# An RNN and an LSTM on one core: x, h0 and bias go out first, weight peaks and splits are put elsewhere among the first 13 steps, and the RNN's split form begins at step 12

## The chip, the core and the metric

The kernel runs on one core of a Trainium2 chip. A core has five engines with queues of their own: TensorE (PE; its weight loads are shown as PEld), VectorE (DVE), ScalarE (ACT), GpSimd (POOL) and SyncE (SP), which here only issues DMAs. ACT issues some DMAs too. An engine works its instructions in order and waits where one asks for a semaphore that has not come. The metric is the device time of one execution in microseconds.

## The reference, cut to what matters

```python
def step(prev_h, xw):                      # RNN, B=32, T=128, D=H=512
    next_h = jnp.tanh(prev_h @ Wh + xw)    # xw = x @ Wx + b
    return (next_h, next_h)
...
def step(carry, xw_t):                     # LSTM, four gates of 512
    prev_h, prev_c = carry
    a = xw_t + prev_h @ Wh
    i, f, o = sigmoid(a[:, :H]), sigmoid(a[:, H:2*H]), sigmoid(a[:, 2*H:3*H])
    g = jnp.tanh(a[:, 3*H:])
    next_c = f * prev_c + i * g
    next_h = o * jnp.tanh(next_c)
    return ((next_h, next_c), next_h)
...
x = x + rnn(x, h0)       # y
x = x + lstm(y, h0)      # c starts at zero
```

## The kernel before

**Steps and lag.** The program is written out by hand, one block for each engine, and each block runs a loop over k = 0 to 133. Iteration k holds step k of the RNN and step k-6 of the LSTM (`LAG = 6`), so the LSTM reads the RNN's sum y six steps later. x is loaded, turned and scaled in groups of four steps (`TG = 4`): group g is steps 4g to 4g+3. The order within an iteration is the order of the calls at the end of each block, and tables with k as the key (`W_HIGH_AT`, `W_LOW_AT`, `PEAK_AT`, `SCALE_AT` and so on) say in which iteration the work on the weights is done.

**Two forms of a product.** In the first steps the products use float32 operands as they were loaded. Later each float32 operand is replaced by two float16 parts, a high and a low one, and a product is three: high by high, high by low, low by high. The LSTM's recurrent product is split from step 1 on (`recurrent_l`), its input product from step 8 on (`product_l`, `S1 = 8`). The RNN's products are split from step `R0` on (`product_r16`, `recurrent_r16`); before, R0 = 8. In the split form one half of the RNN's result comes out in other rows of PSUM, so ACT copies it (`other_half_out`), POOL adds the bias (`add_bias_r16`) and DVE sums (`rnn_add_r16`), and the new h has to be split by ACT and DVE (`rnn_h_hi`, `rnn_h_lo`). In the float32 form DVE adds PSUM and bias directly (`rnn_add`).

**What splitting needs.** Each split takes a scale, a power of two, from a bound on the largest element. For the weights a reduction of each of the four chunks of Wh and Wx of the LSTM (128 x 2048 floats each) gives one column: before, ACT does all eight with Abs and a sum along the row (`weight_peak`). When four are there, TensorE turns them (`turn_peaks`), DVE takes the maximum and puts it on a diagonal (`spread`), TensorE spreads it to all partitions (`spread_peaks`), and DVE works out the scale (`weight_scale`, a chain of short operations). Then ACT writes the high part of each chunk (`weight_high`: `whl_hi`, `wxl_hi`) and DVE the low part (`weight_low`: `whl_lo`, `wxl_lo`). The RNN's weights (`wxr`, `whr`) and each group of x and y are treated likewise. In the profile the exchange goes through `ps_pk`, `peak_col` and `peak_diag`.

**What waits for what.** The recurrent product of LSTM step 1 waits for all four `whl_lo`; the input product of step 8, in iteration 13, waits for all four `wxl_lo` and for y's split (`y_lo`). Step 0 of the LSTM multiplies the raw weights (L729, L737) and needs all eight chunks loaded. The RNN's step r goes TensorE (L788, L798), DVE sum (L634), ACT tanh (L423), DVE turn (L658).

**Loads.** ACT issues x's group 0 as four DMAs, then h0, then the RNN's bias; SP issues `wxr_raw`, `whr_raw`, x group 1, `whl_raw` 0 and 1, x group 2, `whl_raw` 2 and 3, x group 3, four `wxl_raw`, the LSTM's bias and further x.

Of the kernel before, what the change touches and what calls it, by code (L numbers as in the profile page):

```python
# [27 lines left out]
def rnn_lstm_kernel(nc, x, h0, WxR, WhR, bR, WxL, WhL, bL, out):  # L28
# [10 lines left out]
    with ctx:  # L39
# [302 lines left out]
        def _(act):  # L342
            load_x(act, 0)
            act.dma_start(h0n[:, :], h0.rearrange("b (j u) -> j b u", j=J)).then_inc(s_h0, DMA)
            act.dma_start(bias_r[:, :], bass.AP(tensor=bR.tensor, offset=0, ap=[[P, J], [0, B], [1, P]])).then_inc(s_bias_r, DMA)
# [79 lines left out]
            for k in range(END):  # L425
                n, t = k // TG, k % TG
                if 0 <= k - LAG:
                    gate_values(k - LAG)
# [13 lines left out]
                for of, chunk in W_HIGH_AT.get(k, []):  # L442
                    weight_high(of, chunk)
                for of, chunk in W_PEAK_AT.get(k, []):
                    weight_peak(of, chunk)
                for of in R_HIGH_AT.get(k, []):
                    rnn_weight_high(of)
# [478 lines left out]
```

## Time and profile before

| | us |
|---|---|
| median of 3 runs (lowest, highest) | 925.95 (925.73, 926.93) |
| the profiled execution | 926.05 |
| its span in the trace | 924.2 |
| TensorE busy (share of the span) | 866.3 (94%) |
| DVE busy | 754.4 (82%) |
| ACT busy | 409.4 (44%) |
| POOL busy | 233.6 (25%) |

The shares are means over two very different parts. In the last 85% of the span TensorE is busy almost throughout; the first 137 us hold nearly all of its idle time. So the rows to read are those of the start: which engine each one waits for, and when the loads land.

### The profile page before, as it was taken

Reading aid. Unit: us, or ns where it says so; the run is one execution under the profiler, and the core shown is the slowest. Engines: PE = TensorE matmul, PEld = TensorE weight load, DVE = VectorE, ACT = ScalarE, POOL = GpSimd, SP = SyncE. Lnnn points to the kernel's source line nnn. Section 1 sums busy time; section 2 is a strip of 40 time slices with the busy share of each in tenths; the row PEclk is TensorE's granted clock in tenths of the full one; section 3 lists DMA queues with packets and bytes.
Section 4 is the critical chain, followed back from the end, with each engine's and each line's share of the span. In section 5 each row is a group of like instructions: output and inputs, shape, how many; then the busy total and the mean of one; then the engine's idle time right before and its main releaser. Section 6 shows DMA issues by size and latency. Waiting matters only on the chain.

```text
span 924.2 us, 42085 instructions
## 1 busy us (share of the span) xinstructions
PE 866.3 (94%) x18460; PEld 512.9 (55%) x18460; DVE 754.4 (82%) x1985; ACT 409.4 (44%) x1090; POOL 233.6 (25%) x511
## 2 busy tenths in 40 slices
PE   3768779999999999999999999999999999999996
PEld 2524346666565556556555655565556555656542
DVE  3665778888888888888888888888888888888875
ACT  0744444444444444444444544444445444444431
POOL 0221112222222222222222222222222222222210
PEclk9879899999999999999999999999999999999999
DMA  9800000111110001010000010111000100000000
GB/s 312 253 1 2 24 6 23 26 26 26 26 25 24 12 20 26 25 27 26 26 21 19 15 26 26 26 26 26 18 21 17 26 14 15 15 15 15 15 13 13
DMA packets 39328, 30.36 MB, mean 33 GB/s; under 512 B 4328, under 2 KB 37864, under 8 KB 37864
## 3 DMA queue, kind: packets, MB, share of 16 engines
q1 hardware_dynamic: 38304, 27.28, 10.6%
q8 instruction: 144, 2.36, 1.1%
q10 hardware_dynamic: 840, 0.39, 0.2%
q14 instruction: 40, 0.33, 0.1%
HBM read 19.27 MB, written 8.39 MB: 30 GB/s over the span
## 4 chain that ended last, share of the span: by engine, by line
PE 83%; DVE 7%; ACT 4%; issue 3%; DMA 2%; POOL 0%; ACTq 0%; POOLq 0%; DVEq 0%
PE ps_l L750 34%; PE ps_l L774 31%; PE ps_r L813 8%; PE ps_r L830 8%; DMA bias_r<-in_L_cond_b 2%; PE ps_l L763 1%; DVE whl_lo L580 1%; DVE pre_l L593 1%; ACT gates L411 1%; ACT wxl_hi L386 1%; DVE h_hi L615 1%; PE ps_l L729 1%; ACT tanh_c L418 1%; DVE h_lo L625 0%; DVE c L604 0%
## 5 line engine op out<-in xcount | busy, mean ns | idle before, releaser
L774 PE MATMUL ps_l<-wxl_hi,whl_raw 128*32 128x512 f16 x3840 | 251.6, 379 | 2.9 <-issue 2.9
L774 PEld LDWEIGHTS ps_l<-wxl_hi,whl_raw 128*32 128x32 f16 x3840 | 105.6, 97 | 105.1 <-issue 8.3
L307 POOL TENSOR_TENSOR xb<-xb,h_l 128x128 f32<-128x128 f32 x128 | 59.4, 464 | 356.5 <-DVE h_l L621 356.5
L750 PE MATMUL ps_l<-whl_hi,hT_hi 128*32 128x512 f16 x2032 | 134.2, 384 | 11.3 <-DVE whl_lo L580 8.7
L330 POOL TENSOR_TENSOR yT<-xT,hT_r 128x128 f32<-128x128 f32 x128 | 62.8, 491 | 284.5 <-DVE hT_r L658 284.5
L750 PE MATMUL ps_l<-whl_lo,hT_hi 128*32 128x512 f16 x2032 | 133.5, 383 | 0.0
L750 PE MATMUL ps_l<-whl_hi,hT_lo 128*32 128x512 f16 x2032 | 132.6, 381 | 0.0
L593 DVE SCALAR_TENSOR_TENSOR pre_l<-ps_l,g_products,bias_l 128x256 f32<-128x256 f32 x240 | 105.1, 480 | 25.7 <-PE ps_l L750 19.0
L774 PE MATMUL ps_l<-wxl_lo,whl_raw 128*32 128x512 f16 x1920 | 125.8, 379 | 0.0
L641 DVE SCALAR_TENSOR_TENSOR pre_r<-ps_r,g_products,xr 64x128 f32<-64x128 f32 x240 | 84.0, 350 | 41.9 <-POOL xr L320 36.7
L423 ACT ACTIVATE h_r<-pre_r 128x128 f32<-128x128 f32 x128 | 39.6, 310 | 140.6 <-DVE pre_r L641 115.2
L398 ACT ACTIVATE xr<-ps_r,g_products 64x128 f32<-64x128 f32 x120 | 43.8, 365 | 120.5 <-PE ps_r L813 120.5
L407 ACT ACTIVATE hT_r_hi<-hT_r,g_inverses 128x128 f16<-128x128 f32 x120 | 48.2, 402 | 103.6 <-DVE hT_r L658 103.6
L750 PEld LDWEIGHTS ps_l<-whl_lo,hT_hi 128*32 128x32 f16 x2032 | 55.7, 98 | 55.7 <-issue 2.3
L750 PEld LDWEIGHTS ps_l<-whl_hi,hT_lo 128*32 128x32 f16 x2032 | 55.5, 98 | 55.3 <-issue 1.6
L411 ACT ACTIVATE gates<-pre_l 128x256 f32<-128x256 f32 x128 | 53.4, 417 | 73.4 <-DVE pre_l L593 70.2
L625 DVE SCALAR_TENSOR_TENSOR h_lo<-h_l,g_inverses,h_hi 128x128 f16<-128x128 f32 x120 | 77.9, 649 | 4.2
L774 PEld LDWEIGHTS ps_l<-wxl_lo,whl_raw 128*32 128x32 f16 x1920 | 52.7, 97 | 51.4
L750 PEld LDWEIGHTS ps_l<-whl_hi,hT_hi 128*32 128x32 f16 x2032 | 54.1, 98 | 43.0 <-DVE whl_lo L580 9.0
L418 ACT ACTIVATE tanh_c<-c 128x128 f32<-128x128 f32 x128 | 39.7, 310 | 62.1 <-DVE c L604 62.1
L320 POOL TENSOR_TENSOR xr<-xr,bias_r 128x128 f32<-128x128 f32 x120 | 55.1, 459 | 45.4 <-ACT xr L399 42.2
L316 POOL TENSOR_TENSOR xb<-xb,h_r 128x128 f32<-128x128 f32 x128 | 61.0, 476 | 0.0
(97 smaller groups left out, 1286.0 us busy)
## 6 DMA issues: line engine op xcount, KB each, us to landing
out<-xb SPq DMA_DIRECT2D x128, 64.0 KB, 1.8
xb<-in_x SPq DMA_DIRECT2D x124, 64.0 KB, 2.1
whl_raw<-in_L_cond_Wh SPq DMA_DIRECT2D x4, 1024.0 KB, 14.2
wxl_raw<-in_L_cond_Wx SPq DMA_DIRECT2D x4, 1024.0 KB, 18.5
wxr_raw<-in_L_cond_Wx SPq DMA_DIRECT2D x1, 1024.0 KB, 5.4
whr_raw<-in_L_cond_Wh SPq DMA_DIRECT2D x1, 1024.0 KB, 8.0
xb<-in_x ACTq DMA_DIRECT2D x4, 64.0 KB, 8.2
bias_l<-in_L_cond_b SPq DMA_DIRECT2D x4, 64.0 KB, 16.6
```

The costliest lines, as they stand in the source:

```text
L307: nc.gpsimd.tensor_tensor(xb[g % NX][:, t, :], xb[g % NX][:, t, :], h_l[s % 2][:, :], ALU.add).then_inc(out_done, 1)
L316: nc.gpsimd.tensor_tensor(xb[g % NX][:, t, :], xb[g % NX][:, t, :], h_r[r % 2][:, :], ALU.add).then_inc(y_done, 1)
L320: nc.gpsimd.tensor_tensor(xr[r % 2][:, :], xr[r % 2][:, :], bias_r[:, :], ALU.add).then_inc(r16_sum, 1)
L330: nc.gpsimd.tensor_tensor(yT[g % 2][:, :, t, :], xT[g % 2][:, :, t, :], hT_r[:, :, :], ALU.add).then_inc(yT_done, 1)
L411: nc.scalar.activation(gates[:, 0:2 * P], pre_l[:, 0:2 * P], ACT.Sigmoid).then_inc(lstm_act, 1)
L593: nc.vector.scalar_tensor_tensor(out=pre_l[:, cols], in0=ps_l[s % 2][:, cols], scalar=unscale_l(s), in1=bias_l[:, cols], op0=ALU.mult, op1 ...
L625: nc.vector.scalar_tensor_tensor(out=h_lo[:, :], in0=h_l[s % 2][:, :], scalar=factor, in1=h_hi[:, :], op0=ALU.mult, op1=ALU.subtract).then ...
L641: last = nc.vector.scalar_tensor_tensor(out=pre_r[half, :], in0=ps_r[r % 2][half, m * P:(m + 1) * P], scalar=unscale_r[half, g:g + 1], in1 ...
L750: last = nc.tensor.matmul(ps_l[s % 2][quarter(j), :], (hT_hi, hT_lo)[h_part][:, k, :], gate_slice(whl[w_part][k], j), start=False, stop=(h ...
L774: last = nc.tensor.matmul(ps_l[s % 2][quarter(j), :], y16[y_part][g % 2][:, k, t * B:(t + 1) * B], gate_slice(wxl[w_part][k], j), start=(y ...
L813: last = nc.tensor.matmul(ps_r[r % 2][quarter(2 * p + c), 0:2 * P], (hT_r_hi, hT_r_lo)[h_part][:, 2 * p + k, :], quadrant_of_r16(wr[OF_H][ ...
L830: last = nc.tensor.matmul(ps_r[r % 2][quarter(2 * p + c), 0:2 * P], x16[x_part][g % 2][:, 2 * p + k, t * B:(t + 1) * B], quadrant_of_r16(w ...
```

## The change

SP now issues two of the four DMAs of x's group 0 and the RNN's bias ahead of all matrices; ACT issues the other two and h0. R0 becomes 12. The LSTM weights' bounds are shared: chunks 1 and 3 of Wh and chunk 3 of Wx get a maximum on DVE (`weight_max`), the other five stay on ACT (`weight_bound`, the former `weight_peak`). The two scale exchanges of the RNN's groups become one, `scales` loses its partial forms, and its first batch is exchanged in iteration 9, not 5. The spreading matmul of Wh's peaks stands ahead of step 0's recurrent product. ACT's high parts of Wx move ahead of the gates' next use, one of them a step earlier, and DVE's low parts now stand right behind `hidden` (the LSTM's state) and ahead of `rnn_add`, where before they closed the iteration. `whr`'s split moves from k = 3 and 4 to k = 7 and 8.

```diff
-R0 = 8
+R0 = 12
...
-        EXCHANGE = {OF_H: 1, OF_X: 3}
-        R_SCALE_AT = 1
-        SCALE_AT = {OF_H: 4, OF_X: 8}
+        EXCHANGE = {OF_H: 1, OF_X: 2}
+        R_SCALE_AT = 2
+        SCALE_AT = {OF_H: 4, OF_X: 7}
...
+            load_x(sp, 0, (0, 1))
+            sp.dma_start(bias_r[:, :], bass.AP(tensor=bR.tensor, offset=0, ap=[[P, J], [0, B], [1, P]])).then_inc(s_bias_r, DMA)
             sp.dma_start(wr_raw[OF_X][:, :], WxR.rearrange("(p k) n -> p (k n)", k=J)).then_inc(s_wr[OF_X], DMA)
...
-            load_x(act, 0)
+            load_x(act, 0, (2, 3))
             act.dma_start(h0n[:, :], h0.rearrange("b (j u) -> j b u", j=J)).then_inc(s_h0, DMA)
-            act.dma_start(bias_r[:, :], bass.AP(tensor=bR.tensor, offset=0, ap=[[P, J], [0, B], [1, P]])).then_inc(s_bias_r, DMA)
...
+            def weight_max(of, k):
+                dve.wait_ge((s_whl, s_wxl)[of][k], DMA)
+                nc.vector.tensor_reduce(peaks[:, J * of + k:J * of + k + 1], raw[of][k][:, :], mybir.AxisListType.X, ALU.max,
+                                        apply_absolute_value=True).then_inc(w_peaked[of], 1)
...
                     hidden(k - LAG)
...
+                for of, chunk in W_LOW_AT.get(k, []):
+                    weight_low(of, chunk)
+                if k in R_LOW_AT:
+                    rnn_weight_low(R_LOW_AT[k])
                 if LAG <= k < R0:
                     rnn_add(k)
...
-                for of, chunk in W_LOW_AT.get(k, []):
-                    weight_low(of, chunk)
```

DVE in the first steps, before: from the turn of x's group 1 in iteration 0 to the sum of RNN step 2.

```order
L466 STREAM_TRANSPOSE xT<-xb 128x4x4x32
L570 TENSOR_REDUCE peaks<-whr_raw 128x1
L634 TENSOR_TENSOR pre_r<-ps_r,bias_r 128x128
L658 STREAM_TRANSPOSE hT_r<-h_r 128x128
L490 TENSOR_REDUCE peak_col<-ps_pk 2x1
L494 TENSOR_SCALAR peak_diag<-ident,peak_col 2x2
L634 TENSOR_TENSOR pre_r<-ps_r,bias_r 128x128
```

The same stretch of DVE after, to the sum of RNN step 3:

```order
L475 STREAM_TRANSPOSE xT<-xb 128x4x4x32
L643 TENSOR_TENSOR pre_r<-ps_r,bias_r 128x128
L667 STREAM_TRANSPOSE hT_r<-h_r 128x128
L579 TENSOR_REDUCE peaks<-whr_raw 128x1
L643 TENSOR_TENSOR pre_r<-ps_r,bias_r 128x128
L667 STREAM_TRANSPOSE hT_r<-h_r 128x128
L499 TENSOR_REDUCE peak_col<-ps_pk 2x1
L503 TENSOR_SCALAR peak_diag<-ident,peak_col 2x2
L574 TENSOR_REDUCE peaks<-whl_raw 128x1
L643 TENSOR_TENSOR pre_r<-ps_r,bias_r 128x128
```

The maximum of `whr_raw` and the exchange stand one RNN step later, and a maximum of `whl_raw` has come in ahead of the sum of step 3.

DVE in iterations 10 and 11, before, from `hT_lo` of LSTM step 4 to the cell of step 5 (numbers behind a name are buffer numbers):

```order
L628 STREAM_TRANSPOSE hT_lo<-h_lo 128x128
L641 SCALAR_TENSOR_TENSOR pre_r<-ps_r0,g_products,xr0 64x128 x2
L471 SCALAR_TENSOR_TENSOR xT_lo1<-xT1,g_inverses,xT_hi1 128x512
L478 TENSOR_REDUCE peaks<-xb6 128x1
L658 STREAM_TRANSPOSE hT_r<-h_r0 128x128
L580 SCALAR_TENSOR_TENSOR wxl_lo1<-wxl_raw1,w_scale,wxl_hi1 128x2048
L593 SCALAR_TENSOR_TENSOR pre_l<-ps_l1,m_unscale,bias_l 128x256 x2
```

And after:

```order
L637 STREAM_TRANSPOSE hT_lo<-h_lo 128x128
L561 TENSOR_TENSOR g_products<-g_power,factors 128x6x2
L564 RECIPROCAL g_inverses<-g_products 128x6x2
L589 SCALAR_TENSOR_TENSOR wxl_lo1<-wxl_raw1,w_scale,wxl_hi1 128x2048
L643 TENSOR_TENSOR pre_r<-ps_r0,bias_r 128x128
L480 SCALAR_TENSOR_TENSOR xT_lo1<-xT1,g_inverses,xT_hi1 128x512
L487 TENSOR_REDUCE peaks<-xb6 128x1
L667 STREAM_TRANSPOSE hT_r<-h_r0 128x128
L602 SCALAR_TENSOR_TENSOR pre_l<-ps_l1,m_unscale,bias_l 128x256 x2
```

The low part has moved from behind the RNN's turn to ahead of the RNN's sum, which has its float32 form here.

ACT from the tanh of the LSTM's cell in iteration 9, before, to the gates of iteration 10:

```order
L418 ACTIVATE tanh_c<-c 128x128
L398 ACTIVATE xr1<-ps_r1,g_products 64x128
L399 ACTIVATE xr1<-ps_r1,g_products 64x128
L423 ACTIVATE h_r1<-pre_r 128x128
L407 ACTIVATE hT_r_hi<-hT_r,g_inverses 128x128
L386 ACTIVATE wxl_hi0<-wxl_raw0,w_scale 128x2048
L411 ACTIVATE gates<-pre_l 128x256
```

ACT after, from the RNN's tanh of iteration 8 to the one of iteration 9:

```order
L423 ACTIVATE h_r0<-pre_r 128x128
L365 ACTIVATE yT1<-yT1,m_scale 128x512
L386 ACTIVATE wxl_hi0<-wxl_raw0,w_scale 128x2048
L411 ACTIVATE gates<-pre_l 128x256
L413 ACTIVATE gates<-pre_l 128x128
L414 ACTIVATE gates<-pre_l 128x128
L418 ACTIVATE tanh_c<-c 128x128
L386 ACTIVATE wxl_hi1<-wxl_raw1,w_scale 128x2048
L386 ACTIVATE wxl_hi2<-wxl_raw2,w_scale 128x2048
L423 ACTIVATE h_r1<-pre_r 128x128
```

`wxl_hi0` stands one iteration earlier, and two more high parts are done where one was, ahead of the RNN's tanh.

## Rows read from the trace of the kernel before

**Rows 1.** Stretches: bounds and length, busy us (instructions) by engine, clock, DMA share, GB/s

```profile
31.70:42.00 10.30, 7.97 (x99) 4.64 (x99) 6.68 (x9) 7.34 (x8) 3.76 (x4) 0.67 1.02 261
...
53.50:62.20 8.70, 0.01 (x3) 0.00 (x0) 7.74 (x14) 4.71 (x5) 5.18 (x3) 0.69 0.00 0
62.20:137.50 75.30, 61.11 (x929) 31.13 (x933) 46.82 (x120) 30.03 (x63) 11.57 (x25) 0.88 0.04 9
137.50:203.00 65.50, 65.50 (x1460) 42.26 (x1452) 57.24 (x153) 30.40 (x86) 18.22 (x41) 1.00 0.11 27
```

**Rows 2.** TensorE in order of time: start, us, line, operation [idle before <- releaser]

```profile
62.25 1.90 PE L750 MATMUL ps_l<-whl_hi,hT_hi 128*32 128x512 f16 x16 [8.74 <-DVE whl_lo L580]
...
133.59 1.05 PE L774 MATMUL ps_l<-wxl_hi,whl_raw 128*32 128x512 f16 x16 [2.87 <-issue]
...
137.48 1.05 PE L750 MATMUL ps_l<-whl_hi,hT_hi 128*32 128x512 f16 x16
```

**Rows 3.** DMA issues at 1.19, 7.18, 7.65, 16.1: last number us to landing

```profile
whr_raw<-in_L_cond_Wh SPq DMA_DIRECT2D x1, 1024.0 KB, 8.0
...
whl_raw<-in_L_cond_Wh SPq DMA_DIRECT2D x1, 1024.0 KB, 15.2
...
whl_raw<-in_L_cond_Wh SPq DMA_DIRECT2D x1, 1024.0 KB, 18.3
...
wxl_raw<-in_L_cond_Wx SPq DMA_DIRECT2D x1, 1024.0 KB, 22.6
```

**Rows 4.** Queues, 4 to 6 us: packets, MB, share of engines; then DVE's turn of h0

```profile
q1 hardware_dynamic: 110, 0.77, 94.9%
q10 hardware_dynamic: 109, 0.05, 8.5%
...
16.68 0.40 DVE L455 STREAM_TRANSPOSE hT_r<-h0n 128x128 f32<-128x128 f32 x1 [5.06 <-DMA h0n<-in_cond]
```

**Rows 5.** Operations in order of time, all engines, 17 to 58 us

```profile
17.29 2.25 DVE L570 TENSOR_REDUCE peaks<-wxr_raw 128x1 f32<-128x2048 f32 x1
...
24.56 1.89 ACT L381 ACTIVATE whl_lo<-whl_raw 128x2048 bf16<-128x2048 f32 x1
...
27.40 0.13 DVE L528 TENSOR_SCALAR r_peak<-ps_pk 128x2 f32<-128x2 f32 x1
...
28.81 0.23 DVE L500 TENSOR_SCALAR factors<-r_scale,factors 128x2 f32<-128x2 f32 x1
...
37.20 4.86 PE L729 MATMUL ps_l<-whl_raw,h0T 128*32 128x512 f32 x29
...
37.52 1.24 DVE L478 TENSOR_REDUCE peaks<-xb 128x1 f32<-128x512 f32 x2
...
42.41 0.16 DVE L506 TENSOR_REDUCE w_peak<-ps_pk 128x1 f32<-128x4 f32 x1 [0.96 <-PE ps_pk L846]
...
43.64 0.27 DVE L634 TENSOR_TENSOR pre_r<-ps_r,bias_r 128x128 f32<-128x128 f32 x1
...
44.29 0.44 DVE L658 STREAM_TRANSPOSE hT_r<-h_r 128x128 f32<-128x128 f32 x1 [0.38 <-ACT h_r L423]
...
44.66 1.19 DVE L466 STREAM_TRANSPOSE xT<-xb 128x512 f32<-128x512 f32 x1
...
51.22 0.75 DVE L593 SCALAR_TENSOR_TENSOR pre_l<-ps_l,bias_l 128x256 f32<-128x256 f32 x2
...
54.52 0.31 DVE L628 STREAM_TRANSPOSE hT_lo<-h_lo 128x128 f16<-128x128 f16 x1
...
57.42 4.78 DVE L580 SCALAR_TENSOR_TENSOR whl_lo<-whl_raw,w_scale,whl_hi 128x2048 f16<-128x2048 f32 x2
```

**Rows 6.** Waits, 88 to 137 us (us in total, times, longest); and ACT's high part

```profile
DVE wxl_lo L580 <- ACT wxl_hi L386: 8.8, 4, 2.4
...
107.70 1.99 ACT L386 ACTIVATE wxl_hi<-wxl_raw,w_scale 128x2048 f16<-128x2048 f32 x1
```

**Rows 7.** An add on POOL while DVE writes `wxr_lo`

```profile
31.79 2.47 POOL L330 TENSOR_TENSOR yT<-xT,hT_r 128x128 f32<-128x128 f32 x1 [3.35 <-DVE hT_r L658]
```

More of the change, by code:

```diff
@@ L429, in _ @@
                     cell_tanh(k - LAG)
+                    for of, chunk in W_BOUND_AT.get(k, []):
+                        weight_bound(of, chunk)
+                    if k in R_HIGH_AT:
+                        rnn_weight_high(R_HIGH_AT[k])
+                    if k >= SCALE_AT[OF_X] + 2:
+                        for of, chunk in W_HIGH_AT.get(k, []):
+                            weight_high(of, chunk)
                 if R0 <= k < T:
@@ L441, in _ @@
                     y_scale(Y_SCALE_AT[k])
[L442 to L447, printed above, removed]
+                if k < SCALE_AT[OF_X] + 2:
+                    for of, chunk in W_HIGH_AT.get(k, []):
+                        weight_high(of, chunk)
+                if k < LAG:
+                    for of, chunk in W_BOUND_AT.get(k, []):
+                        weight_bound(of, chunk)
+                if k < LAG and k in R_HIGH_AT:
+                    rnn_weight_high(R_HIGH_AT[k])
         @block.vector
@@ L547, in x_power, with scales @@
                                         ALU.bitwise_and).then_inc(done, 1)
-            def scales(i, kinds, done, step):
+            def scales(i, done, step):
                 first, count = BATCHES[i]
-                cols, shape = slice(first, first + count), [P, kinds.stop - kinds.start, count]
-                nc.vector.tensor_tensor(g_products[:, kinds, cols], g_power[:, cols].unsqueeze(1).broadcast_to(shape),
-                                        factors[:, kinds].unsqueeze(2).broadcast_to(shape), ALU.mult).then_inc(done, 1)
+                cols, shape = slice(first, first + count), [P, 6, count]
+                nc.vector.tensor_tensor(g_products[:, :, cols], g_power[:, cols].unsqueeze(1).broadcast_to(shape),
+                                        factors[:, :].unsqueeze(2).broadcast_to(shape), ALU.mult).then_inc(done, 1)
                 dve.wait_ge(done, step + 1)
-                nc.vector.reciprocal(g_inverses[:, kinds, cols], g_products[:, kinds, cols]).then_inc(done, 1)
+                nc.vector.reciprocal(g_inverses[:, :, cols], g_products[:, :, cols]).then_inc(done, 1)
             def x_scale(i):
@@ L666, in _ @@
                     rnn_add(k)
+                    for of, chunk in W_LOW_FIRST_AT.get(k, []):
+                        weight_low(of, chunk)
                     rnn_turn(k)
+                    if k == 0:
+                        turn_x(1)
+                    if k in R_PEAK_AT:
+                        rnn_weight_peak(R_PEAK_AT[k])
+                    if k == R_SCALE_AT:
+                        spread(EXCHANGE_R, 2)
+                    if k - 1 == R_SCALE_AT:
+                        rnn_weight_scale()
+                    if k in W_MAX_AT:
+                        weight_max(*W_MAX_AT[k])
+                    if k == SCALE_AT[OF_H]:
+                        spread(EXCHANGE[OF_H], J)
+                        weight_scale(OF_H)
                 if 0 <= k - LAG:
```

118 lines of the change are left out of this document (49 added, 69 removed).

## The prediction

> **What bounds the kernel now.** I read the table of stretches first [rows 1]. From 137.5 to 203 us TensorE is busy all of 65.50 us at the full granted clock; before that it is not. From 62.2 to 137.5 it works 61.11 of 75.30 us at a mean clock of 0.88, and from 53.5 to 62.2 it does nothing. So the program has a TensorE-bound tail and a start in which others decide. The next view, TensorE's own rows [rows 2], gives the marks: LSTM step 1 begins its recurrent product at 62.25, after 8.74 us in which it waited for the last `whl_lo`; the first split input product (step 8) begins at 133.59, and the recurrent product of step 8 at 137.48. From there both kernels issue the same work in the same order, at TensorE's pace. The question is thus when that product starts; 924.2 - 137.48 = 786.7 us follow it unchanged. The landing rows [rows 3] and the durations [rows 5] let me walk the new order up to it. I count iterations k as the code does: k carries RNN step k and LSTM step k-6.
>
> **1. x, h0 and bias first.** Before, h0 is only turned at 16.68, after DVE waited 5.06 us for it [rows 4], though its descriptors were out by 4.06. The two rows of the DMA queues from 4 to 6 us say why: queue 10 (ACT's) and queue 1 (SP's) moved 109 and 110 packets, one for one, and queue 1's have 8 KB. After the change h0 is issued third instead of fifth on ACT's queue, some 1.2 us earlier, and the matrices some 1.5 us later (three small issues of about 0.5 us ahead of them). x0 no longer shares its way. I take h0 landed at about 10, when `whr_raw` lands too: it was 1.19 + 8.0 = 9.2 [rows 3], and I add 0.8, between 0 (x0, h0 and bias use time in which the DMA engines were idle) and the 1.5 of the issue. RNN step 0 then multiplies at 10 to 11.3 rather than behind 16.68: 6 us sooner. But most of that is not kept. `whl_raw2` landed at 7.18 + 15.2 = 22.4, and the same bytes are ahead of it; with +0.3 (bounds 0 and +1.5) it lands at 22.7, and ACT's bound on it sits in front of the tanh of RNN step 3. So the first term is a landing: 22.7.
>
> **2. Peaks and scales of the LSTM weights, k = 3 to 4.** From 22.7: ACT's bound 1.89 + 0.19 [rows 5] to 24.8. The tail of RNN step 3 (tanh, turn) 0.75 to 25.55. The scale of the RNN weights, six dependent short operations from 27.40 to 29.04 in the rows, 1.65 to 27.2. `weight_max` of chunk 3 on DVE: the nearest row is the reduction of `wxr_raw`, 2048 columns too, 2.25, to 29.45 (`whl_raw3` is there from 7.65 + 18.3 + 0.3 = 26.3). Chunk 1's maximum, done by 23.9, ends before ACT does. Moving three of eight peaks to DVE thus costs DVE 2.25 here and saves ACT 2.08; before, all four of Wh were on ACT, one after another. The tail of RNN step 4 takes 1.1 (43.64 to 44.73), to 30.55; largest of a column and diagonal 0.55, to 31.1; TensorE spreads it, 0.4; the weight scale takes 1.3 (42.41 on), to 32.9. The spread now stands ahead of step 0's product, so the scale no longer waits for it: 42.41 becomes 31.6.
>
> **3. Step 0 and the splits of Wh, k = 4 to 6.** TensorE multiplies step 0's recurrent part from 31.6. In the rows it took 5.2 with the granted clock at 0.67 around it [rows 1, 5]; TensorE has been waiting since about 26.7 for two microseconds and more, so I keep the slow value, to 36.8 (at full clock 3.6, as the same 32 matmuls of the input part took; at 1.2 GHz throughout twice that, 7.3). RNN step 5: product 0.9 to 37.7, sum to 38.05. Meanwhile DVE does `wxr_lo` (33.0 to 35.3), which is hidden. Then `whl_lo0` 2.35 to 40.4, turn to 40.8, `whl_lo1` and `whl_lo2` to 45.6 with 0.2 of waiting (ACT's three high parts follow each other at 1.92 from 39.0). `wxl_raw3` lands at 16.1 + 22.6 + 0.3 = 39.0, so step 0's input product ends at 42.2 and is hidden. LSTM step 0 takes from 51.22 to 54.83 in the rows, 3.6: to 49.2. `whl_lo3` 2.35: 51.6. **The recurrent product of step 1 starts at 51.6, not 62.25: 10.65 us sooner.**
>
> **4. The splits of Wx, k = 7 to 13.** Step 1's product waits 4.1 us before it starts, so I keep the slow clock and 5.1 (2.7 at full clock): DVE's cell 1 at 56.75. From here I give the starts of the cell on DVE. Cell to `hT_lo` is 3.7.
> k=7: `weight_max` 2.25, RNN sum, x peak 0.65 (1.24 for two), turn, to 64.1; TensorE's own work, with the turned peaks waiting for 62.75, ends step 2's product at 65.8. Cell 2 at 65.85.
> k=8: 3.7, weight scale 1.35, `whr_lo` 2.3, then sum, peak, turn 1.4: cell 3 at 74.6.
> k=9: ACT does `wxl_hi0` ahead of the gates: +1.5; spread 0.5, `wxl_lo0` 2.35, x turn 1.15, sum, peak, turn 1.4, x power 0.6: cell 4 at 85.75 (11.15).
> k=10: 3.75, scales 0.35, low part 2.35, sum, `xT_lo` 0.7, peak, turn: 94.25.
> k=11: 3.75 + 2.35 + 1.35: 101.7.
> k=12: 3.75, spread 0.5, low part 2.35 to 108.3; RNN's first split sum, `y_lo`, turn, x power: cell 7 at 111.2. Input product of step 8 starts behind `y_lo` at 110.2; RNN's low half comes at 113.35 and TensorE reaches the recurrent product of step 8 at **114.4**.
> What makes this shorter is one wait: before, each of k=9 to 12 had ACT's high part (1.99) after ACT's `hT_r_hi`, and DVE idle for it: four waits, 2.4 the longest, 8.8 us in all [rows 6]. Now the high part lies a step ahead of the low part. R0 = 12 takes four steps off the longer path through ACT, GpSimd and the low half (0.4 + 0.35 of DVE each), and costs TensorE about 0.5 us in each of four steps, which DVE's 7.5 to 11 us a step hide.
>
> GpSimd and DVE: an add on GpSimd that takes 0.46 alone took 2.47 beside `wxr_lo` [rows 7]. At k=12 the bias add starts at 106.5, inside `wxl_lo3`, so I end it at 108.7 instead of 107.0; since DVE itself is free at 108.3, that is 0.4 in the sum. In the Trainium skill, SBUF — State Buffer, section SBUF: two separate sides, the pair of ports that the two share is a lock held for a whole instruction, and the loser stands still. By that rule the long operations next to the LSTM state speak against this change; by it the time is 903.0, without it 902.6.
>
> **The sum.** 137.48 - 114.4 = 23.1. The profiled execution: 924.2 + 1.85 around it = 926.05, 0.1 over the median of 925.95. 926.05 - 23.1 = 903.0.
>
> **The rivals.**
> *A, the walk as it stands*: 901 to 906. For it: every length is a row and 137.5 on is full.
> *B, the granted clock stays up at step 0 and at step 1*: 1.6 and 2.4 less, 899.0. For it: less waiting than now. Against: it fell in each of the early stretches with a wait of some 2 us or more.
> *C, h0 late*: if it again takes 12.6 us from its descriptors (16.68 - 4.06), it lands at 15.5; RNN step 0 starts 5 us later than I say, the slack of about 0.6 at the tanh of step 3 is gone and that comes at 29.3: +4.2, 907.2. For it: the one-for-one row. Against: x0 is out of its queue's way. The Trainium skill, DMA: Bandwidth & Descriptors, section Queues, rings and completion order, has the DMA engines take turns between queues by packets, so that small ones beside a matrix stay slow even when issued first.
> *D, more waits than I walked*: loads late by the full 1.5 (+1.2), step 0 at 1.2 GHz throughout (+2.1) and one more clock fall inside k = 7 to 12 (+2.5): up to 909.
> *E, half the gain*: another engine's queue (ACT at k = 6 and 7, with 4 to 6 us of long work before the tanh) delays every early step: about 915.
> *F, slower*: the loop from step 8 on locks with DVE later than TensorE. There are 120 steps, so from 0.19 us each the 23 us are gone; at 0.3 the time is 903.0 + 36 = 939. Against: 65.50 of 65.50 busy, and DVE 57.24 of it: it can catch up 1 us in a step.
>
> **How the numbers follow.** A 0.50, B 0.15, C 0.15, D 0.14, E 0.03, F 0.02, and 0.01 that it all ends even. About 0.2% is what a measurement of this kernel can tell from no change. A, B, C and most of D hold over 8 in 10: from 898.5 to 909.5. Faster 0.97, same 0.01, slower 0.02.
>
> **What would show it.** h0 turned at about 10; tanh of RNN step 3 at 25 right behind ACT's bound; the weight scale at 31.6 ahead of step 0's product; step 1's product at 51.6; no DVE wait for `wxl_hi`; cells 7.5 to 11 us apart; step 8's recurrent product at 114.4 with TensorE full after it. Wrong if a long wait of DVE on ACT stands in k = 6 to 9, if landings move by over 2 us, or if TensorE is not full after 115.

## The result, and the profile after

| | before | after |
|---|---|---|
| median of 4 runs (lowest, highest), us | 926.44 (925.73, 926.96) | 899.19 (897.55, 900.53) |
| ratio (95% interval) | | 0.9706 (0.9687 to 0.9724) |
| the profiled execution, us | 926.05 | 900.53 |
| its span, us | 924.2 | 898.7 |
| TensorE busy, us (share) | 866.3 (94%) | 861.6 (96%) |

The change saves 27 us. The forecast was 903.0 (898.5 to 909.5): 3.8 above the median, 2.5 above the profiled execution. The runs of the changed kernel lie up to 3 us apart, and the profiled one is the slowest of the four, so the traces are compared below from marks inside them, and the medians where a time is meant.

The stretches of the changed kernel (bounds and length, busy us (instructions) by engine, granted clock, DMA share, GB/s) answer to [rows 1]:

```profile
26.00:37.00 11.00, 7.53 (x92) 3.96 (x96) 8.16 (x20) 5.02 (x6) 1.76 (x4) 0.69 1.04 369
47.50:53.00 5.50, 1.07 (x44) 0.80 (x39) 4.84 (x11) 4.94 (x8) 0.56 (x1) 0.99 0.01 1
53.00:108.00 55.00, 52.82 (x900) 27.35 (x900) 45.57 (x109) 23.78 (x44) 10.20 (x19) 0.97 0.05 12
112.00:203.00 91.00, 91.00 (x2028) 58.98 (x2023) 80.27 (x213) 42.24 (x120) 25.52 (x57) 1.00 0.10 26
```

From 112 us TensorE is busy all of the time, as it was before from 137.5. Between LSTM step 1 and step 8 it now works 52.82 of 55.00 us at a clock of 0.97, where it had worked 61.11 of 75.30 at 0.88.

TensorE's rows in order of time (start, us, line, operation, idle before and its releaser) answer to [rows 2]:

```profile
13.34 1.94 PE L809 MATMUL ps_r<-whr_raw,hT_r 128*32 128x128 f32 x32 [1.15 <-DMA whr_raw<-in_L_cond_Wh]
...
33.29 4.90 PE L740 MATMUL ps_l<-whl_raw,h0T 128*32 128x512 f32 x32
...
52.97 1.90 PE L761 MATMUL ps_l<-whl_hi,hT_hi 128*32 128x512 f16 x16 [4.43 <-DVE whl_lo L589]
...
108.10 1.05 PE L785 MATMUL ps_l<-wxl_hi,whl_raw 128*32 128x512 f16 x16 [0.43 <-DVE whl_raw L492]
...
111.99 1.05 PE L761 MATMUL ps_l<-whl_hi,hT_hi 128*32 128x512 f16 x16
```

Step 1's recurrent product starts at 52.97 instead of 62.25, and its wait is 4.43 instead of 8.74. Step 8's starts at 111.99 instead of 137.48: 25.49 us sooner, and the profiled executions are 25.52 apart. Nothing was gained or lost after that mark. Of the 25.5 us, 9.3 are there by step 1 and 16.2 come between step 1 and step 8 (59.0 us instead of 75.2). Three kernels of the experiments have the same code up to step 1 (R0 = 16, and the two with the parts of Wx put back); there its product starts at 50.89, 51.21 and 50.59, so 52.97 is a late case.

The landings (last number: us from issue to landing) answer to [rows 3]; `whr_raw` is issued at 2.87, the second `whl_raw` pair from 9.82 on. Behind them stands the turn of h0 on DVE, which answers to [rows 4], and ACT's bound on chunk 2 with the tanh of RNN step 3 behind it:

```profile
wxr_raw<-in_L_cond_Wx SPq DMA_DIRECT2D x1, 1024.0 KB, 7.8
whr_raw<-in_L_cond_Wh SPq DMA_DIRECT2D x1, 1024.0 KB, 10.4
```

```profile
8.31 0.40 DVE L464 STREAM_TRANSPOSE hT_r<-h0n 128x128 f32<-128x128 f32 x1 [3.41 <-DMA h0n<-in_cond]
```

```profile
24.50 1.91 ACT L381 ACTIVATE whl_lo<-whl_raw 128x2048 bf16<-128x2048 f32 x1 [1.96 <-DMA whl_raw<-in_L_cond_Wh]
...
26.41 0.29 ACT L423 ACTIVATE h_r<-pre_r 128x128 f32<-128x128 f32 x1
```

h0 is there at 8.31 instead of 16.68, but now `whr_raw` is what RNN step 0 waits for, and it lands at 2.87 + 10.4 = 13.3, not at 9.2. `wxr_raw`, ahead of it, already took 7.8 us instead of 5.4. The tanh of step 3 stands right behind ACT's bound, at 26.41 (30.98 before).

### The profile page after: what moved, and what is told of

Same layout as the page of the kernel before. It is cut to its first block, busy times and chain, and to the rows that moved or that the text cites. A ratio compares the mean times of both kernels' runs of the same rounds, so it can differ in the third digit from the quotient of the medians.

```text
span 898.7 us, 42172 instructions
## 1 busy us (share of the span) xinstructions
PE 861.6 (96%) x18524; PEld 510.3 (57%) x18524; DVE 755.4 (84%) x1977; ACT 398.7 (44%) x1071; POOL 228.4 (25%) x507
## 4 chain that ended last, share of the span: by engine, by line
PE 84%; DVE 8%; issue 2%; ACT 2%; DMA 2%; SPq 1%; POOL 0%; POOLq 0%; ACTq 0%; DVEq 0%
PE ps_l L761 35%; PE ps_l L785 31%; PE ps_r L824 8%; PE ps_r L841 8%; DMA whl_raw<-in_L_cond_Wh 2%; DVE pre_l L602 1%; ACT gates L411 1%; DVE whl_lo L589 1%; DVE h_hi L624 1%; DVE h_lo L634 1%; SPq L263 1%; ACT tanh_c L418 1%; DVE c L613 1%; DVE fc L609 1%; DVE ig L611 1%
## 5 line engine op out<-in xcount | busy, mean ns | idle before, releaser
L331 POOL TENSOR_TENSOR yT<-xT,hT_r 128x128 f32<-128x128 f32 x128 | 58.6, 458 | 295.5 <-DVE hT_r L667 295.5
L650 DVE SCALAR_TENSOR_TENSOR pre_r<-ps_r,g_products,xr 64x128 f32<-64x128 f32 x232 | 81.1, 350 | 34.8 <-POOL xr L321 29.8
## 6 DMA issues: line engine op xcount, KB each, us to landing
whl_raw<-in_L_cond_Wh SPq DMA_DIRECT2D x4, 1024.0 KB, 14.2
whr_raw<-in_L_cond_Wh SPq DMA_DIRECT2D x1, 1024.0 KB, 10.4
```

Of the source, the lines that this page charges most:

```text
L331: nc.gpsimd.tensor_tensor(yT[g % 2][:, :, t, :], xT[g % 2][:, :, t, :], hT_r[:, :, :], ALU.add).then_inc(yT_done, 1)
L650: last = nc.vector.scalar_tensor_tensor(out=pre_r[half, :], in0=ps_r[r % 2][half, m * P:(m + 1) * P], scalar=unscale_r[half, g:g + 1], in1 ...
```

## The experiments

Of the causes, I had named one wait (`wxl_lo` on `wxl_hi`, 8.8 us [rows 6]), the loads, the spread put ahead and the shared bounds; to R0 = 12 I had given 0.4 + 0.35 us of DVE a step, some 3 us in all, and had taken its cost on TensorE to be hidden. The runs undo each alone, or do one alone. Not tried alone are the move of `whr`'s split to k = 7 and 8 and the joining of the RNN's exchanges. Where a saving "from the mark" is given, it is the time from the recurrent product of step 1 to DVE's cell of step 8 in the trace (the cell starts with the add that reads the gates' sums, `pre_l`): 78.3 us before, 62.4 after. It leaves out the loads' scatter. Differences to the changed kernel are of the medians. The kernel before ran beside each group of experiments too, at 925.83, 926.97 or 926.38 us; by the ratios to it the differences come out up to 0.9 us otherwise (2.0 in place of 2.9 for the bounds on ACT).

### The loads, undone and alone

The changed kernel with the old loads:

```diff
-            load_x(sp, 0, (0, 1))
-            sp.dma_start(bias_r...)
-            load_x(act, 0, (2, 3))
+            load_x(act, 0)
             act.dma_start(h0n...)
+            act.dma_start(bias_r...)
```

> The changed kernel with the loads of x's group 0, h0 and bias as before (all on ACT's queue, matrices first on SP's). My theory: h0 is turned at about 16.7 again instead of 8.3, RNN step 0's recurrent product starts at about 17.2 instead of 13.3, and since only some 0.7 us of slack stand ahead of ACT's bound on chunk 2 of Wh, 3 to 4 us of that reach the end: 902 to 903 against the changed kernel's 899.2. Rival (the landing of chunk 2 sets the start whatever the RNN does): tanh of RNN step 3 stays within 1 us of 26.4, time 898 to 900. Rival (the load order is the main thing): over 8 us back, 907 or more.

Measured: 903.16 (902.26 to 905.2), ratio 0.9754 (0.9739 to 0.9768). That is 4.0 over the changed kernel, a little above the 902 to 903 that were expected. The other way round, the kernel before with the new loads and nothing else:

> The kernel before with the new order of loads alone (x's group 0 on both queues, bias on SP, nothing else). My theory: the RNN starts 4 us sooner and all of it is kept up to step 1 of the LSTM, since that start bounded the kernel before: 922 us (921 to 924) against 926.4. Rival (loads are throughput-bound and give nothing): 925.5 to 926.5. Rival (main thing): 915 or less.

Measured: 920.81 (918.7 to 923.81), ratio 0.9944 (0.9927 to 0.996): 5.0 less than the kernel before beside it, and just below the 921 to 924 expected. So the loads are worth 4 to 5 us either way. With the old loads in the changed kernel, RNN step 0 waits for h0 as before (TensorE's rows):

```profile
17.23 1.94 PE L808 MATMUL ps_r<-whr_raw,hT_r 128*32 128x128 f32 x32 [3.21 <-DVE hT_r L463]
...
56.81 1.90 PE L760 MATMUL ps_l<-whl_hi,hT_hi 128*32 128x512 f16 x16 [4.43 <-DVE whl_lo L588]
```

Step 0 starts 3.9 us later than in the changed kernel and step 1 of the LSTM 3.8 us later: the whole delay is handed on. Against the three earlier cases named above (RNN step 0 at 11.6 to 12.2) both delays are 5.0 to 6.2 us. In the kernel before with new loads, step 1's product comes at 56.78 instead of 62.25, with the same 8.72 of waiting for `whl_lo`.

### R0 = 12 alone

```diff
-R0 = 8
+R0 = 12
...
-        BATCHES = [(RG, 2)] + [(g, 4) for g in range(4, NG, 4)]
+        BATCHES = [(G1, 2)] + [(g, 4) for g in range(4, NG, 4)]
```

(in the kernel before; the two waits on `x_peaked` count from G1 too.)

> The kernel before with R0 = 12 alone (groups 2 and 3 of x still scaled in one early batch, which is then batch 2, 2). My theory: in k = 8 to 11 the RNN's float32 sum does without ACT's copies, the bias add, ACT's and DVE's split of h, 1.5 to 2 us of each of four iterations that DVE bounds: 918 to 921 against 925.8. Rival (TensorE pays 0.5 us a step and the rest is hidden): 925.5 to 928.

Measured: 915.82 (914.89 to 917.5), ratio 0.9883 (0.9868 to 0.9897). That is 11.1 us less than the kernel before beside it (926.97), against the 5 to 8 expected. Iteration 9 shows how. DVE in the kernel before, from the cell of step 3 on:

```profile
87.78 0.87 DVE L593 SCALAR_TENSOR_TENSOR pre_l<-ps_l,m_unscale,bias_l 128x256 f32<-128x256 f32 x2
...
93.25 0.71 DVE L641 SCALAR_TENSOR_TENSOR pre_r<-ps_r,g_products,xr 64x128 f32<-64x128 f32 x2 [1.47 <-POOL xr L320]
...
98.41 2.35 DVE L580 SCALAR_TENSOR_TENSOR wxl_lo<-wxl_raw,w_scale,wxl_hi 128x2048 f16<-128x2048 f32 x1 [2.36 <-ACT wxl_hi L386]
```

and the same operations with R0 = 12 alone:

```profile
83.60 0.88 DVE L593 SCALAR_TENSOR_TENSOR pre_l<-ps_l,m_unscale,bias_l 128x256 f32<-128x256 f32 x2 [1.28 <-PE ps_l L750]
...
87.93 0.29 DVE L634 TENSOR_TENSOR pre_r<-ps_r,bias_r 128x128 f32<-128x128 f32 x1 [0.33 <-PE ps_r L798]
...
90.49 2.42 DVE L580 SCALAR_TENSOR_TENSOR wxl_lo<-wxl_raw,w_scale,wxl_hi 128x2048 f16<-128x2048 f32 x1 [0.27 <-ACT wxl_hi L386]
```

From the cell to the start of `wxl_lo0` it was 10.63 us and is 6.89. The wait for POOL (1.47) becomes one of 0.33 for TensorE, because no copy by ACT and no add by POOL lie between product and sum. The wait for `wxl_hi` falls from 2.36 to 0.27, though ACT's high part stands where it stood: ACT no longer has to do `hT_r_hi` ahead of it. The stretches from cell to cell (k = 9, then the five of k = 8 to 12 together as 58.42 us before and 47.41 after; of the kernel before, then of this one) give the rest:

```profile
87.78:100.79 13.01, 11.23 (x176) 5.75 (x168) 8.73 (x20) 4.54 (x9) 1.91 (x4) 1.00 0.17 42
...
sum 58.42, PE 44.53 PEld 22.92 DVE 39.23 ACT 24.77 POOL 9.36; mean PE 8.91 PEld 4.58 DVE 7.85 ACT 4.95 POOL 1.87
```

```profile
83.60:92.83 9.23, 9.23 (x160) 4.36 (x156) 8.00 (x17) 3.42 (x6) 3.09 (x3) 1.00 0.18 45
...
sum 47.41, PE 40.07 PEld 21.67 DVE 35.90 ACT 19.54 POOL 9.63; mean PE 8.01 PEld 4.33 DVE 7.18 ACT 3.91 POOL 1.93
```

DVE's work falls by 3.3 us, as the 0.4 + 0.35 a step had it, and its idle time from 19.2 to 11.5, by 7.7, for which I had no term. By iteration, from k = 8 to 12, the five are 3.1, 3.8, 2.8, 1.2 and 0.1 us shorter. Of the 8.8 us for which `wxl_lo` waited, 5.0 are left with R0 = 12 alone.

Two things stand outside these stretches. LSTM step 1's product already starts at 60.68 instead of 62.25: DVE's low part of x's group 2, with a wait of 0.68 ahead of it, is gone from iteration 6. And at step 8's input product the granted clock fell, which it had not done in the kernel before. Here are TensorE's rows for it, first of the kernel before with the new loads, then of this one:

```profile
128.14 1.05 PE L776 MATMUL ps_l<-wxl_hi,whl_raw 128*32 128x512 f16 x16 [3.50 <-issue]
```

```profile
121.54 1.90 PE L774 MATMUL ps_l<-wxl_hi,whl_raw 128*32 128x512 f16 x16 [3.50 <-issue]
```

Both waited 3.50 us for the same product; the clock was 1.00 from 128 to 130 us in the first and 0.50 from 122 to 124 in the second.

### How long the float32 form should last

```diff
-R0 = 12
+R0 = 16
```

> The changed kernel with R0 = 16. In iterations 12 to 15 the RNN's products stay float32: 1.75 us of TensorE a step instead of 1.31, and no split of h. My theory: at k = 12 DVE still bounds and saves 1 us, at k = 13 to 15 TensorE bounds and pays 0.44 each plus the first product: 899.2 to 900.5. Rival (the float32 form is the better one as long as it can be had, as it was in k = 8 to 11): 897 or less.

Measured: 899.58 (898.71 to 900.96), ratio 0.9713 (0.9694 to 0.9731). No difference that the runs can tell. From step 1's product to the end its trace takes 846.1 us instead of 845.7. Past step 12 the low parts of Wx are done, and from 112 us TensorE is full in the changed kernel.

### The low and the high parts of Wx, where they stood before

First only the low parts, in the changed kernel: those of k = 9 to 12 back at the end of the iteration.

```diff
-                for of, chunk in W_LOW_AT.get(k, []):
+                for of, chunk in W_LOW_AT.get(k, []) if k < 9 else []:
                     weight_low(of, chunk)
...
                     x_power(BATCH_AT.index(k))
+                for of, chunk in W_LOW_AT.get(k, []) if k >= 9 else []:
+                    weight_low(of, chunk)
```

> The changed kernel with DVE's four low parts of Wx back at the end of their iterations (k = 9 to 12), while ACT's high parts keep their early place. My theory: what the change gains there is the wait of DVE for ACT, not the place of the low part, so DVE has the same sum of work in each iteration and the time stays within 1 us of 899.2. Rival (the place right behind the LSTM state is what gains): each of four iterations pays 1 us or more, 903 or more. Rival (the place costs, since it holds back the RNN): 898 or less.

Measured: 903.34 (903.12 to 903.54), ratio 0.9752 (0.974 to 0.9765): 4.1 us more than the changed kernel, where I expected none. Each part of it has a row. At k = 10 ACT's high part of x was covered by DVE's low part, and is waited for now; at k = 12 the last low part comes to stand behind `y_lo`, so TensorE waits for it (DVE's rows, then TensorE's two, of this kernel):

```profile
88.60 0.75 DVE L480 SCALAR_TENSOR_TENSOR xT_lo<-xT,g_inverses,xT_hi 128x512 f16<-128x512 f32 x1 [0.71 <-ACT xT_hi L356]
...
106.18 2.62 DVE L589 SCALAR_TENSOR_TENSOR wxl_lo<-wxl_raw,w_scale,wxl_hi 128x2048 f16<-128x2048 f32 x1
```

```profile
108.91 1.60 PE L787 MATMUL ps_l<-wxl_hi,whl_raw 128*32 128x512 f16 x16 [1.99 <-issue]
110.25 1.96 PE L787 MATMUL ps_l<-wxl_lo,whl_raw 128*32 128x512 f16 x16
```

The product of step 8 starts when `wxl_lo3` ends (106.18 + 2.62 = 108.80). After the 1.99 us of waiting its groups of 16 take 1.60, 1.96 and 1.41 us instead of 1.05. The granted clock of this kernel from 100 to 112 us is 0.89, while in the changed kernel, whose wait there was 0.43, it is 1.00. From the mark this kernel takes 66.4 us instead of 62.4. The rows account for it: 0.7 of waiting at k = 10, 1.6 more of it ahead of step 8's product, and 1.8 for its three groups at the lower clock. So less than half of the 4.1 us is the clock, which after such a wait falls in some kernels and in others not (R0 = 12 alone, above).

Then the high parts back too, one each at k = 9 to 12 and all behind the RNN's tanh (the line of the table; the calls move as well):

```diff
-... 8: [(OF_X, 0)], 9: [(OF_X, 1), (OF_X, 2)], 10: [(OF_X, 3)]}
+... 9: [(OF_X, 0)], 10: [(OF_X, 1)], 11: [(OF_X, 2)], 12: [(OF_X, 3)]}
```

> The changed kernel with both parts of Wx's split as before: ACT's high parts behind the RNN's tanh in k = 9 to 12, DVE's low parts at the end of the same iterations. My theory: DVE waits 1.6 us for ACT in k = 9 and 10 and 2.3 in k = 11 and 12, less the 1.5 that the early high part now holds back the gates in k = 9: +6.4 (5 to 9), 904 to 908. Rival (place of the low part matters, lead does not): the same as the run with the low parts alone put last.

Measured: 905.37 (904.28 to 906.91), ratio 0.9778 (0.9765 to 0.9791): 6.2 more than the changed kernel, inside what was expected. Three of the four waits are back (DVE's rows, k = 10 to 12):

```profile
89.39 2.35 DVE L585 SCALAR_TENSOR_TENSOR wxl_lo<-wxl_raw,w_scale,wxl_hi 128x2048 f16<-128x2048 f32 x1 [0.41 <-ACT wxl_hi L386]
...
98.83 2.35 DVE L585 SCALAR_TENSOR_TENSOR wxl_lo<-wxl_raw,w_scale,wxl_hi 128x2048 f16<-128x2048 f32 x1 [2.36 <-ACT wxl_hi L386]
...
109.42 2.35 DVE L585 SCALAR_TENSOR_TENSOR wxl_lo<-wxl_raw,w_scale,wxl_hi 128x2048 f16<-128x2048 f32 x1 [1.72 <-ACT wxl_hi L386]
```

They make 4.5 us. I had expected 7.8 of such waits, less 1.5 at the gates; so the time was met, but not by its parts, and that is partly luck. Both places together are worth 6.2 us, and with the early high parts kept, putting the low parts back alone gives 4.1 of them away. The high parts back alone were not tried.

### The spreading matmul behind step 0's product

```diff
-                if k == SCALE_AT[OF_H]:
-                    spread_peaks(EXCHANGE[OF_H], J)
                 if k == STEP_0_AT:
                     step_0_recurrent()
+                if k == SCALE_AT[OF_H]:
+                    spread_peaks(EXCHANGE[OF_H], J)
```

> The changed kernel with the spreading matmul of Wh's peaks behind step 0's recurrent product, as before. My theory: the scale comes at 38.2 instead of 33.4, the low part of wxr is then no longer hidden and the sum of RNN step 5 waits behind it, so the first low part of Wh starts 3 us later and all of that reaches the end: 902.2 (901 to 903.5). Rival (step 0's product and RNN step 5 bound that stretch, the scale does not): within 1 us of 899.2.

Measured: 901.89 (901.03 to 902.53), ratio 0.973 (0.9716 to 0.9743): 2.7 more. The scale of the weights waits for TensorE (DVE's row):

```profile
36.50 0.16 DVE L515 TENSOR_REDUCE w_peak<-ps_pk 128x1 f32<-128x4 f32 x1 [5.15 <-PE ps_pk L857]
```

In the changed kernel that row is at 33.39 with 1.30 of waiting. From ACT's bound on chunk 2 to step 1's product it is 30.2 us here and 28.5 in the changed kernel, so the traces show 1.8 of the 2.7.

### All bounds on ACT

`W_MAX_AT` is empty, and chunks 1 and 3 of Wh and 3 of Wx are bounded by ACT at k = 2, 3 and 7.

```diff
-        W_MAX_AT = {2: (OF_H, 1), 3: (OF_H, 3), 7: (OF_X, 3)}
+        W_MAX_AT = {}
```

> The changed kernel with all eight bounds of the LSTM weights on ACT again, in the same iterations. My theory: the tanh of RNN step 4 waits 1.0 us longer behind ACT's longer queue and that of step 7 1.9 us, of which some 0.5 reach the cell: 900 to 902. Rival (sharing the bounds is the main source of what the loads and the order at k = 9 to 12 don't explain): 905 or more.

Measured: 902.06 (900.7 to 902.62), ratio 0.9728 (0.9715 to 0.9742): 2.9 more (2.0 by the ratios), just over the 900 to 902 expected. The tanh of RNN step 3 comes at 27.89 instead of 26.41, that of step 4 at 32.80 instead of 30.72, and the product of LSTM step 1 at 54.70 instead of 52.97. But this execution also got its loads late: RNN step 0 starts at 14.22, not 13.34, and ACT's bound on chunk 2 waits for the landing until 25.99, not 24.50:

```profile
25.99 1.91 ACT L382 ACTIVATE whl_lo<-whl_raw 128x2048 bf16<-128x2048 f32 x1 [1.66 <-DMA whl_raw<-in_L_cond_Wh]
```

From there to step 1's product it is 28.7 us against 28.5, and from that mark on the two kernels take the same (62.5 and 62.4 us). So of the 1.7 us between the traces 1.5 are the landing and 0.2 the edit, and moving the chunk of Wx shows nothing. The medians say more, and the runs do not overlap (900.7 at least against 900.53 at most), but the 95% intervals of the ratios do. What sharing the bounds is worth, between 0.2 and 2.9 us, stays open.

### The granted clock at steps 0 and 1

Here matmuls are added, whose result is read by nothing, in the stretches where TensorE waits: ahead of step 1's product, in iteration 4, and ahead of the turn of the peaks.

```diff
+            def keep_busy(n, out):
+                for _ in range(n):
+                    nc.tensor.matmul(out[0:B, 256:512], h0T[:, 0:B], wr_raw[OF_X][:, 0:256], start=True, stop=True)
```

The first version has 32, 12 and 16 of them:

> The changed kernel with 60 small float32 matmuls added on TensorE whose result nothing reads: 12 and 16 around RNN step 4's product in iteration 4, 32 while it waits for the split of Wh ahead of LSTM step 1. My theory: the granted clock stays at 1.00 in both waits, step 0's recurrent product takes 3.5 instead of 4.9 us and step 1's 2.7 instead of 4.4, both in front of what DVE waits for: 3.2 us less, 896 (895 to 897.5). Rival (the clock falls for other reasons, or added matmuls delay as much as they save): 899 or more.

Measured: 912.31 (911.59 to 912.74), ratio 0.9842 (0.9828 to 0.9855): 13 us more, where 896 was expected. TensorE's rows:

```profile
29.64 7.07 PE L867 MATMUL ps_l<-wxr_raw,h0T 128*32 128x256 f32 x32
...
38.05 3.64 PE L740 MATMUL ps_l<-whl_raw,h0T 128*32 128x512 f32 x32
```

A float32 matmul shows as two passes here. The 16 ahead of the turn are 32 passes of 256 columns and took 7.07 us, 0.22 each; I had sized them from step 0's, where 32 passes of 512 columns take 3.64, 0.11 each. So the filler was longer than the waits, and step 0 began at 38.05 instead of 33.29. But step 0 took 3.64 instead of 4.90, as the theory had it. With 9, 3 and 4 instead:

> As the run with 60 added matmuls, with 16 instead (3 and 4 in iteration 4, 9 ahead of LSTM step 1). There each pass took 0.22 us, twice what I had counted, and the queue overran both waits, but the clock stayed at 1.00 and step 0's product took 3.64. Sized to the waits: 18 passes of 0.22 = 3.9 us in the wait of 4.4, 8 in that of 2.3, 6 in that of 1.7. My theory: clock stays up, 1.3 and 1.7 us come back in front of what DVE waits for: 896.2 (895 to 897.5). Rival (the work added still delays, or the clock falls all the same): 899 or more.

Measured: 895.59 (895.04 to 896.96), ratio 0.9669 (0.9652 to 0.9687): 3.6 less than the changed kernel. TensorE's rows:

```profile
32.64 3.64 PE L740 MATMUL ps_l<-whl_raw,h0T 128*32 128x512 f32 x32
...
47.21 4.05 PE L867 MATMUL ps_pk<-wxr_raw,h0T 128*32 128x256 f32 x18
...
51.09 1.04 PE L761 MATMUL ps_l<-whl_hi,hT_hi 128*32 128x512 f16 x16
51.96 1.04 PE L761 MATMUL ps_l<-whl_lo,hT_hi 128*32 128x512 f16 x16
```

Both products run at the full clock: step 0 in 3.64 and the first groups of step 1 in 1.04 where they had 1.90. The clock is at 1.00 from 24 to 60 us. This is the price of the two clock falls that the forecast kept: in the traces 1.9 us are there by step 1's product, 1.3 of them in step 0's own, and 1.7 come behind its start.

### x's group 2 behind all chunks of Wh, as group 3 is

```diff
-            load_x(sp, 2)
             load_chunk(whl_raw[2][:, :], WhL, 2, s_whl[2])
             load_chunk(whl_raw[3][:, :], WhL, 3, s_whl[3])
+            load_x(sp, 2)
             load_x(sp, 3)
```

> The changed kernel with x's groups 2 and 3 issued behind all four chunks of Wh, so that chunk 2 has 0.26 MB in 512-byte pieces less ahead of it. My theory: chunk 2 of Wh lands 1.3 to 2 us sooner than 24.5, the RNN's own chain then binds after 0.7 us of slack, and 0.7 us reach the end: 898.5 (897.5 to 899.2). Rival (the landing bounds everything up to step 1): 897.5 or less. Rival (landings are not in the chain): 899.2.

Measured: 899.71 (897.33 to 900.74), ratio 0.9709 (0.9688 to 0.973): alone it makes no difference that the runs can tell, where 898.5 was expected. ACT's rows show why:

```profile
21.61 1.89 ACT L381 ACTIVATE whl_lo<-whl_raw 128x2048 bf16<-128x2048 f32 x1
...
25.16 0.31 ACT L423 ACTIVATE h_r<-pre_r 128x128 f32<-128x128 f32 x1 [1.56 <-DVE pre_r L643]
```

The bound has no wait for its chunk any more, but the tanh of step 3 waits 1.56 us for DVE's sum: the RNN's own chain, which began when `whr_raw` landed, is next. The tanh is 12.2 us behind the start of RNN step 0's product, where it was 13.1: 0.9 less, of which the time shows nothing. With the added matmuls as well:

> Both of the former edits together. If they act on different waits, as I think, their gains add: 895.5 (894.5 to 897).

Measured: 894.75 (894.23 to 895.01), ratio 0.9659 (0.9642 to 0.9675). This is the fastest version of all, 4.4 us under the changed kernel and 0.8 under the one with the added matmuls alone. The intervals of these two overlap, so the 0.8 is not shown.

## Why the prediction was right, step by step

**The bound, and what follows it.** Right. TensorE is full after the mark, nothing changes there, and rival F (a loop locked with DVE) and rival E (half the gain) fell: 91.00 of 91.00 us busy from 112 on.

**1. The loads.** The mechanism was right, two sizes were not. h0 was turned at 8.31 (I said 10), so C, h0 late, fell. That rival had leaned on the Trainium skill, DMA: Bandwidth & Descriptors, section Queues, rings and completion order, which says that a DMA engine takes turns between queues packet by packet. That small transfers beside a matrix stay slow even when issued first was my conclusion from it. Here h0, with its descriptors out at 3.06, came in 5.25 us instead of 12.6, and all eleven traces with the new loads turn it between 5.84 and 8.96, the three with the old loads between 16.68 and 16.83. The turns themselves are not refuted: from 2 to 4 us the two queues now moved 285 and 373 packets (56 and 63 before), because queue 1 had small ones too at that time. The slowness passed to the matrices: `whr_raw` landed at 13.3, not at 10. The step that failed is the bound that x0, h0 and bias "use time in which the DMA engines were idle": `whr_raw` was issued 1.68 later and then took 10.4 instead of 8.0. The term that I used, chunk 2 of Wh, was missed by less: 24.5 instead of 22.7. In the three kernels with the same code up to step 1 it was 22.35 to 22.86, so that the 22.7 was good and the profiled execution late. ACT's bound was indeed right ahead of the tanh of step 3. It was 26.41 instead of 24.8.

**2. Peaks and scales.** Right apart from that delay: the scale chain began at 33.39 (31.6), as step 0's product started and not behind it, and 7.0 us behind the tanh (6.8 in the walk). Undoing the spread cost 2.7; undoing the shared bounds cost 2.9 by the medians, of which the trace shows 0.2.

**3. Step 0 and the splits of Wh.** Right: 4.90 at the slow clock (I said 5.2), and then 19.68 us from step 0's product to step 1's (the walk: 20.0). So the 1.4 by which 52.97 lies over 51.6 come from the landing. Case A stood, with the clock falling at both waits. Case B's price of 1.6 + 2.4 = 4.0 came out as 3.6. The reason given against B, that the clock fell in each early stretch with a wait of some 2 us, is too strong: ahead of step 8's product the kernel before waited 2.87 us, and with the new loads 3.50, and the groups behind took 1.05 both times.

**4. The splits of Wx.** Here the size was off by 3.8 us in the other direction: 59.0 us from step 1's product to step 8's, not 62.8. That is as much as the forecast lies over the median; the profiled execution comes 1.4 us closer because its step 1 was that late. Step 1's product took 4.5 to the cell and not 5.15, because only its first two groups ran slow: in the rows 52.97 + 1.90, then 1.88, then 1.03. The iterations k = 8 to 12 were each 0.4 to 1.1 us shorter than walked (10.01, 7.95, 6.95 and 9.12 for k = 9 to 12, where I had 11.15, 8.5, 7.45 and 9.5). In part durations had been added that overlap: the operations of k = 11 on DVE each start 0.08 us before the one ahead has ended:

```profile
96.37 2.31 DVE L589 SCALAR_TENSOR_TENSOR wxl_lo<-wxl_raw,w_scale,wxl_hi 128x2048 f16<-128x2048 f32 x1
98.60 0.28 DVE L643 TENSOR_TENSOR pre_r<-ps_r,bias_r 128x128 f32<-128x128 f32 x1
98.80 0.67 DVE L487 TENSOR_REDUCE peaks<-xb 128x1 f32<-128x512 f32 x1
99.39 0.40 DVE L667 STREAM_TRANSPOSE hT_r<-h_r 128x128 f32<-128x128 f32 x1
99.71 0.44 DVE L602 SCALAR_TENSOR_TENSOR pre_l<-ps_l,m_unscale,bias_l 128x256 f32<-128x256 f32 x1
```

Durations of these five make 4.10 us, first start to last end is 3.78. That is 0.3 of the 0.5 by which k = 11 was shorter. At k = 9 terms were also too long in themselves: x power took 0.21 instead of 0.6, and sum, peak and turn 1.10 instead of 1.4. The +1.5 for `wxl_hi0` ahead of the gates was right: DVE waited 1.51 us for ACT's gates there.

**What was put down to the wrong cause.** "What makes this shorter is one wait" did not hold. No wait for `wxl_hi` is left, as I said, but the walk had counted iterations in their new form, and the sentence gave all of it to the place of the high parts. Alone, R0 = 12 gives 11.1 us and already removes 3.8 of the 8.8; both places of the parts of Wx give 6.2, and of that the low parts' place gives 4.1, for which no term stood in the prediction. The time came out right because the walk adds operations and waits along DVE's own row and needs no attribution. The parts as measured are loads 4.0, R0 = 12 11.1, places 6.2, spread 2.7, bounds 2.9: together 26.9 of 27.2. R0 was measured in the kernel before and the others in the changed one (R0 = 8 there was not run), falls of the clock are counted in R0's and in the places', two parts of the change were not tried, and the 2.9 is not sure. So that the sum closes is luck in good part.

**GpSimd beside DVE.** The bias add of k = 12 (POOL's row) was stretched, but by less than the 2.2 that I gave it:

```profile
104.87 1.54 POOL L321 TENSOR_TENSOR xr<-xr,bias_r 128x128 f32<-128x128 f32 x1 [1.47 <-ACT xr L399]
```

It took 1.54 instead of 0.46 and ended at 106.41, 0.32 behind `wxl_lo3` (103.76 + 2.33). With this the rule of the Trainium skill, SBUF — State Buffer, section SBUF: two separate sides, agrees: the loser stands still until the other is done. What it cost on DVE's row was forecast as 0.4 and is 0.36, in front of `y_lo`, for which step 8's product waits:

```profile
106.45 0.71 DVE L650 SCALAR_TENSOR_TENSOR pre_r<-ps_r,g_products,xr 64x128 f32<-64x128 f32 x2 [0.36 <-POOL xr L321]
```

How much of it reached the end was not tried.

## What to carry to other kernels

Walk the engine that is waited for, operation by operation, rather than add up the waits that an edit removes: a wait has several parents, and another edit may have taken most of it away already. A dependent chain through three engines (copy, add, sum) inside an iteration costs its waits on the next long operation as well, so look at its length first where TensorE is idle anyway. Where a long operation moves, check the last iteration, in which its consumer comes: `wxl_lo3` behind `y_lo` cost a wait of 2 us and, in that run, the clock. Where two traces are compared, first take off what their loads differ by: of the 1.7 us that seemed to belong to the shared bounds, 1.5 were a late landing.

## What the runs showed of the hardware

- The added float32 passes of 256 columns, all into the same 32 rows of PSUM, took 0.22 us each, and step 0's passes of 512 columns, which go round four groups of rows, 0.11 each, both at the full clock. Whether the rows are the cause was not tried apart.
- Sixteen such matmuls (32 passes) in three waits hold the granted clock at 1.00 through both products and are worth 3.6 us. A wait of 1.99 us ahead of step 8's product was followed by groups at 1.60 and 1.96 us, one of 0.43 by groups at 1.05. The length of the wait alone does not decide it: after 3.50 us one kernel's first group took 1.90 us (R0 = 12 alone) and another's 1.05 (the kernel before with the new loads).
- The column of the granted clock does not show every slow product. In the changed kernel the RNN's products of steps 0 and 1, 32 passes each, took 1.94 and 1.93 us and that of step 2 only 1.08, while the column reads 1.00 from 10 to 28 us. The lengths of equal groups are the surer sign.
- With the small transfers ahead of the matrices the second matrix landed at 13.3 us instead of 9.2. It took 8.7 to 11.3 us from its issue in the eleven traces with these loads, and 8.0 to 8.2 in the three with the old ones. TensorE starts RNN step 0 between 11.6 and 14.2 us among the kernels with the same first loads. This is of the size of the spread between the runs of one kernel, but it is not its only source: the kernel before, where RNN step 0 waits for h0 and starts at 17.2, spreads as much (924.79 to 927.93 in nine runs).
